# Second attention in a pipeline of four steps instead of three, and the work at its borders placed anew

## What is computed

```python
x = x + tanh(g_xattn[0]) * L0_xattn(layernorm(x), ctx)             # one head, softmax(q k^T / sqrt(128)) v
x = x + tanh(g_ffn[0])   * L0_ffn(layernorm(x), ...)               # 8 experts 128->256->128, relu, top 2 by softmax
x = x + tanh(g_xattn[1]) * L1_xattn(layernorm(x), ctx, ctx, mask)  # 16 heads of 8, biases, output projection
x = x + tanh(g_ffn[1])   * L1_ffn(layernorm(x), ...)               # 8 experts of 96 and a shared one, silu, top 2 by sigmoid
```

## Time and profile before

| | us |
|---|---|
| median of 3 runs | 766.39 (763.78, 766.39, 766.4) |
| the profiled execution | 767.7 |
| its span, first to last instruction | 765.9 |
| stage a | 0 to 136 |
| stage b | 136 to 376 |
| stage c | 376 to 616 |
| stage d | 616 to 765.9 |

### The profile page before, as it was taken

How to read it: one execution, slowest core, us unless ns; L and a number is a source line. 1 busy time by engine, 2 the same in 40 slices (tenths; PEclk the granted TensorE clock), 3 DMA queues, 4 the chain that set the end, 5 groups by cost and what they waited for, 6 DMA issues and landing times.

```text
span 765.9 us, 12807 instructions
## 1 busy us (share of the span) xinstructions
PE 649.0 (85%) x4078; PEld 503.5 (66%) x4078; DVE 560.2 (73%) x1281; ACT 426.0 (56%) x665; POOL 104.2 (14%) x133
## 2 busy tenths in 40 slices
PE   5865654979999999979599988988988489999996
PEld 3644443657787787757377666766756267888884
DVE  3567565687898898868478668668676669888885
ACT  3333321467777777756277666656766145555553
POOL 3444230020000000000401022022022100000000
PEclk8677665889999999999799999999999679999998
DMA  5312000000000000010244124224210000000000
GB/s 159 101 63 98 29 8 0 1 0 1 1 0 0 0 0 0 0 43 28 50 121 121 54 67 119 69 49 119 69 42 2 0 1 0 15 14 14 27 14 28
DMA packets 23698, 29.24 MB, mean 38 GB/s; under 512 B 3313, under 2 KB 17522, under 8 KB 23666
## 3 DMA queue, kind: packets, MB, share of 16 engines
q1 hardware_dynamic: 23666, 28.84, 13.1%
HBM read 19.99 MB, written 8.85 MB: 38 GB/s over the span
## 4 chain that ended last, share of the span: by engine, by line
PE 63%; DVE 18%; issue 6%; POOL 5%; ACT 5%; DMA 1%; DVEq 1%; SPq 0%; POOLq 0%; ACTq 0%
PE psum L371 12%; PE psum L373 11%; PE psum L372 11%; PE psum L1187 6%; PE psum L1202 3%; PE psum L1177 2%; DVE stats L281 2%; POOL rstd L293 2%; PE psum L360 2%; PE psum L1178 2%; DVE b_hl L811 2%; DVE xn L300 2%; DVE c_mx L1356 2%; PE psum L1503 2%; PE psum L319 1%
## 5 line engine op out<-in xcount | busy, mean ns | idle before, releaser
L371 PE MATMUL psum<-xh,w_hi 128*128 (+1 forms) x248 | 104.1, 420 | 5.2 <-DVE w_lo L1346 3.0
L1297 ACT ACTIVATE c_pt<-psum 77x512 f32<-77x512 f32 x128 | 74.5, 585 | 49.9 <-PE psum L1187 49.8
L372 PE MATMUL psum<-xl,w_hi 128*128 (+1 forms) x248 | 100.3, 404 | 0.0
L373 PE MATMUL psum<-xh,w_lo 128*128 (+1 forms) x248 | 100.1, 404 | 0.0
L930 ACT ACTIVATE b_hr<-psum,b1s 128x512 f32<-128x512 f32 x128 | 80.8, 686 | 24.0 <-PE psum L373 23.9
L978 DVE TENSOR_TENSOR b_hs<-b_hr,psum 128x1024 f32<-128x1024 f32 x64 | 77.9, 1217 | 21.7 <-ACT b_hr L930 20.4
L811 DVE TENSOR_TENSOR b_hl<-b_hs,b_hh 128x1024 fp32r<-128x1024 f32 x64 | 78.3, 1223 | 16.9 <-ACT b_hh L805 16.9
L805 ACT ACTIVATE b_hh<-b_hs 128x1024 fp32r<-128x1024 f32 x64 | 67.9, 1061 | 34.1 <-PE psum L373 32.2
L1187 PE MATMUL psum<-ident,c_pf 128*77 128x128 f32 x512 | 75.9, 286 | 0.0
L1187 PEld LDWEIGHTS psum<-ident,c_pf 128*77 128x77 f32 x512 | 59.4, 152 | 14.9 <-issue 10.4
L1302 ACT ACTIVATE c_pf<-c_sm,zero_col,exp_scale 128x616 f32<-128x616 f32 x64 | 57.3, 895 | 17.8 <-DVE c_sm L1362 17.8
(11 more groups left out here) (207 smaller groups left out, 1299.6 us busy)
## 6 DMA issues: line engine op xcount, KB each, us to landing
w_hi<-c_q_spread SPq DMA_DIRECT2D x24, 256.0 KB
stage<-in_weights SPq DMA_DIRECT2D x8, 576.0 KB, 4.2
c_q_spread<-w_hi SPq DMA_DIRECT2D x7, 512.0 KB, 3.4
ctxg<-in_ctxT SPq DMA_DIRECT2D x16, 156.0 KB, 4.1
c_k_spread<-w_lo SPq DMA_DIRECT2D x8, 312.0 KB, 2.2
x_all<-in_x SPq DMA_DIRECT2D x8, 256.0 KB, 2.7
out_dram<-x_all SPq DMA_DIRECT2D x8, 256.0 KB, 2.3
c_kb<-c_k_spread SPq DMA_DIRECT2D x48, 39.0 KB
```

Source lines behind the costliest of these rows:

```text
L371: pe.matmul(o, wh, h, start=start, stop=False)
L372: pe.matmul(o, wh, l, start=False, stop=False)
L373: return pe.matmul(o, wl, h, start=False, stop=stop)
L1297: a_.activation(pt[:, q % NC4, :], bank[2 + q % 2][0:S2, :], ACT.Copy).then_inc(pt_done, 1)
```

## The change

In stage c a fourth step is added: `step(a, m, t, u)`, u being the group before t. Turning the norm, high and low part, logits, their copy, turning and copy move from parts 13 to 15 of t to parts 1 to 6 of u. `project` goes ahead of the scores of part 9, `residual` to part 9, the statistics are divided over parts 11 (`dve_spread`) and 12 (`dve_moments`). `turn_out` waits in addition for the logits copy of the group before, since both use M1. In the last step but one `act_sigmoid` moves to part 6, `route.first` to part 7 and `route.second` to part 12; `route.weights` goes to part 2 of the last step. `pipeline4` writes out four steps ahead and three behind a loop of two turns; SP's and POOL's steps only take the fourth argument. In stage a, last step: the low part before `route.second`, and the late setup (with bank 5) on all three engines. In stage b, first step: the tail's routing in eight portions (two operations for `pick_part` 0 and 1, one for 2), the ratio at expert 6. In the last full step of stage b: the early preparation at experts 0 and 2 (PE) and 1 and 3 (ACT, DVE), y turned back and residual at 5, norm at 6; at the stage's end ACT copies the norm's high part before the values. No arithmetic is added or left out.

```diff
@@ -95,6 +95,19 @@
     step(None, None, Group(None, NG - 1))
+def pipeline4(eng, step):
+
+    def groups(i, c):
+        return [Group(i, c - k) if c - k >= 0 and (i is not None or c - k < NG) else None for k in range(4)]
+    for c in range(4):
+        step(*groups(None, c))
+    with eng.Fori(0, (NG - 4) // 2) as i:
+        step(*groups(i, 4))
+        step(*groups(i, 5))
+    for c in range(NG, NG + 3):
+        step(*groups(None, c))
+
+
 class Link:
@@ -284,6 +297,19 @@
                     ins = v.bn_aggr(m[:, p, t, :], st[:, p, t, :])
                 ins.then_inc(self.stats_ready, 1)
+            def dve_spread(self, v, g):
+                st, p = self.bufs[0], g.parity
+                for t in range(TG):
+                    ins = v.bn_stats(st[:, p, t, :], x_all[:, g.tile(t), :])
+                ins.then_inc(self.chain, 1)
+
+            def dve_moments(self, v, g):
+                st, m, p = self.bufs[0], self.bufs[1], g.parity
+                wait_apart(v, self.chain, g.at(1, 1))
+                for t in range(TG):
+                    ins = v.bn_aggr(m[:, p, t, :], st[:, p, t, :])
+                ins.then_inc(self.stats_ready, 1)
+
             def pool_rstd(self, q, g):
                 _, m, ve, rs, _ = self.bufs
                 p = g.parity
@@ -429,12 +455,12 @@
         def act_setup_late(a):
             a.wait_ge(s_m0, 2)
-            a.activation(bo_all[:], bank[7][:, 0:P], ACT.Copy, scale=tg[:, 1:2]).then_inc(s_m0e, 1)
+            a.activation(bo_all[:], bank[5][:, 0:P], ACT.Copy, scale=tg[:, 1:2]).then_inc(s_m0e, 1)
         def pe_setup_late(pe):
             pe.wait_ge(s_dve_setup, 1)
-            pe.matmul(bank[7][:, 0:P], bv1[:].broadcast_to([P, P]), wo1[:], start=True, stop=False)
-            pe.matmul(bank[7][:, 0:P], ones_row[:], bo1[:], start=False, stop=True).then_inc(s_m0, 1)
+            pe.matmul(bank[5][:, 0:P], bv1[:].broadcast_to([P, P]), wo1[:], start=True, stop=False)
+            pe.matmul(bank[5][:, 0:P], ones_row[:], bo1[:], start=False, stop=True).then_inc(s_m0, 1)
         def act_split(a_, a):
@@ -550,6 +576,8 @@
                     if t.i is None and t.c == 0:
                         pe.wait_ge(s_split, 1)
                     lg0.pe_product(pe, t)
+                    if not m:
+                        pe_setup_late(pe)
                     lg0.pe_transpose(pe, t)
             pipeline(pe, step)
         pe_parts.append(pe_a)
@@ -578,6 +606,7 @@
                 if t:
                     lg0.act_copy(a_, t)
                     if not m:
+                        act_setup_late(a_)
                         Route(0, HEAD, rt_tail).act_ratio(a_)
             pipeline(a_, step)
         act_parts.append(act_a)
@@ -614,7 +643,6 @@
                         v.wait_ge(s_small, 16 * len(small))
                         v.wait_ge(lg0.lg_copied, NG - 1)
                         route.first(v)
-                        route.second(v)
                 if a:
                     if not (a.i is None and a.c < 2):
                         v.wait_ge(ln0.t_ready, a.at(1, -1))
@@ -632,6 +660,8 @@
                 if t:
                     ln1.dve_low(v, t)
                     if not m:
+                        route.second(v)
+                        dve_setup_late(v)
                         route.weights(v)
                     lg0.dve_copy(v, t)
             pipeline(v, step)
@@ -664,15 +694,23 @@
...
+            def pick_part(self, v, k, values, best, onehot):
+                if k == 0:
+                    link(v, v.tensor_reduce(best, values, AX.X, ALU.max))
+                    link(v, v.tensor_tensor(rt["pick"][:], values, self.bc(best), ALU.is_ge))
+                if k == 1:
+                    link(v, v.tensor_tensor(rt["tmp"][:], rt["pick"][:], rankb, ALU.mult))
+                    link(v, v.tensor_reduce(r1["c"], rt["tmp"][:], AX.X, ALU.max))
+                if k == 2:
+                    link(v, v.tensor_tensor(onehot, rt["tmp"][:], self.bc(r1["c"]), ALU.is_equal))
+
+            def pick(self, v, values, best, onehot):
+
+                for k in range(3):
+                    self.pick_part(v, k, values, best, onehot)
...
@@ -890,18 +943,15 @@
                 for e in range(E if m else LAG):
                     if m:
                         up(m, e)
-                    if m and e == 4 and t:
+                    if m and e == (4 if a else 5) and t:
                         y_back(a, m, t)
                     g, k = xb.prev(m, t, e, LAG)
                     if g:
                         down(g, k)
-                    if m and not a and e < 2:
-                        c_prepare["pe"](pe, e)
+                    if m and not a and e in (0, 2):
+                        c_prepare["pe"](pe, e // 2)
                     if m and e == 2 and a:
                         place(a)
-                    if m and e == 5 and xb.first(m):
-                        pe.wait_ge(xb.st_done, 2)
-                        pe_setup_late(pe)
                     if m and e == 7 and t:
                         ln2.pe_transpose(pe, t)
                 if not m:
@@ -939,12 +989,10 @@
                         g, k = xb.prev(m, t, e)
                         if g:
                             xb.act_high(a_, g, k)
-                        if xb.first(m) and e == 3:
+                        if xb.first(m) and e == 6:
                             tail.act_ratio(a_)
-                        if xb.first(m) and e == 6:
-                            act_setup_late(a_)
-                        if not a and e in (1, 2):
-                            c_prepare["act"](a_, e - 1)
+                        if not a and e in (1, 3):
+                            c_prepare["act"](a_, e // 2)
                         if e == 3 and a:
                             xb.act_place(a_, a, MISC)
                         if e == 7 and t:
@@ -955,8 +1003,8 @@
                     if t:
                         xb.act_high(a_, t, E - 1)
                         xb.act_y(a_, t, Y)
+                        ln2.act_high(a_, t)
                         c_prepare["act"](a_, 2)
-                        ln2.act_high(a_, t)
             pipeline(a_, step)
         act_parts.append(act_b)
@@ -964,9 +1012,23 @@
             tail = Route(0, TAIL, rt_tail)
             def route_last(e):
-                if e == 1:
+                if e == 0:
                     v.wait_ge(lg0.lg_copied, NG)
-                (tail.first, tail.second, tail.weights)[e // 2](v)
+                    tail.values = logits[:, TAIL, :]
+                first = tail.values, tail.r1["m"], rt_tail["first"][:]
+                second = rt_tail["wt"][:], tail.r1["m2"], rt_tail["second"][:]
+                if e < 3:
+                    tail.pick_part(v, e, *first)
+                if e == 2:
+                    tail.mask_first(v)
+                if 3 <= e < 6:
+                    tail.pick_part(v, e - 3, *second)
+                if e == 5:
+                    tail.difference(v)
+                if e == 6:
+                    tail.shares(v)
+                if e == 7:
+                    tail.split(v)
             v.wait_ge(s_pool, 2)
@@ -991,16 +1053,14 @@
                             low(g, k)
                         if e == 0 and a:
                             xb.dve_place(v, a)
-                        if xb.first(m) and e in (1, 3, 5):
+                        if xb.first(m):
                             route_last(e)
-                        if xb.first(m) and e == 4:
-                            dve_setup_late(v)
-                        if not a and e in (1, 2):
-                            c_prepare["dve"](v, e - 1)
-                        if e == 4 and t:
+                        if not a and e in (1, 3):
+                            c_prepare["dve"](v, e // 2)
+                        if e == (4 if a else 5) and t:
                             xb.dve_residual(v, t, MISC)
                             ln2.dve_stats(v, t)
-                        if e == 5 and t:
+                        if e == (5 if a else 6) and t:
                             ln2.dve_norm(v, t)
                         if e == 7 and t:
                             ln2.dve_low(v, t)
@@ -1214,6 +1274,8 @@
             def turn_out(t):
                 pe.wait_ge(o_done, t.at(TG, TG))
+                if not (t.i is None and t.c == 0):
+                    pe.wait_ge(lg1.lg_copied, t.at(1, 0))
                 for b in range(TG):
...
@@ -1254,6 +1316,8 @@
                     g, q = lagged(m, t, i - 3)
                     if g:
                         transpose(g, q)
+                    if t and i == 9:
+                        project(t)
                     if m and i % 2 == 1 and i < NQ - 1:
                         scores(m, (i + 1) // 2)
                     if a and i == NQ - 1:
@@ -1262,16 +1326,14 @@
                         prepare(a, i // 3)
                     if a and m and i == 6:
                         prepare_values(a)
```

(57 more changed lines are left out.)

46 lines of the change are left out of this document (26 added, 20 removed).

## The result

The changed kernel takes 745.65 us (median of 6 runs, 743.24 to 748.15), the kernel before, run beside it, 765.21 (6 runs, 763.5 to 767.48). The ratio is 0.974 with a 95% interval of 0.971 to 0.977. The profiled execution of the changed kernel took 744.32 us with a span of 742.5, that of before 767.7 with 765.9.

The account below looks back on a forecast made before the run. TensorE (PE), busy 85% of the span, bounds the kernel through its pauses and lower clock. Gains 0 + 7.7 + 5.0 + 1.1 + 10.2 = 24.0 us gave 743.7, 742.4 against the median, 743.5 with one clock fall; range 736 to 753.

Parts of the forecast that it names:

- The likeliest case: Whole kernel: the main forecast of 743.5 us, given a chance of 0.62.
- End of stage a: Last step of the first attention: low part sooner, but PE waits for the moved setup; cost 0.2 us, taken as 0.
- an earlier rise of the clock: End of the first attention: PE busy without a pause from 134.0 may bring the clock up earlier, giving 0.6 us back.
- First expert step: Stage b's first step: without setup and bunched routing PE reaches the next group's first product at 160.8; gain 7.7 us.
- Rival (B): First expert step: DVE becomes the bound, half of the 7.7 us is lost, 747.4 us; chance 0.07.
- Last expert step and the border: End of stage b: PE's 2.99 us wait goes, gain 5.0; ACT's high part ahead of the values, gain 1.1 us.
- the new wait at the norm's turning: Last expert step: norm at expert 6 makes PE wait 1.6 us more at the turning of expert 7.
- Second attention: Stage c: full steps of 26.4 us, five taking 132.0 instead of 139.8; gain of the whole part 10.2 us.
- Rival (A): Second attention: full steps gain nothing, new stalls replace those removed; 752.5 us, chance 0.20 shared with Rival (C).
- Rival (C): Second attention: the clock falls in every step, six more falls of 1.4 us; 752 us, chance 0.20 shared with Rival (A).
- The 1.0 us that I added for one fall: Second attention: allowance of 1.0 to 1.4 us for one fall of the clock, raising the forecast to 743.5 us.

Follow-up runs that it names:

- e3: Changed kernel with the late setup put back into the first expert step, routing still in eight portions and the ratio at expert 6: 747.31 us, ratio 0.975.
- e4: Changed kernel with the tail's routing in three bunches again and ACT's ratio at expert 3, late setup kept at the end of stage a: 752.23 us, ratio 0.982.
- e9: Changed kernel with ACT copying the values ahead of the norm's high part again at the end of stage b: 748.57 us, ratio 0.977.
- e1: Changed kernel with the three-step stage c of the kernel before put back, border work in stages a and b kept: 758.62 us, ratio 0.990.
- e5: Changed kernel, still four steps, with residual and all statistics together at part 10 and the projection behind the scores of part 9: 746.07 us, ratio 0.975.
- e6: e1 with the split statistics, residual at 9 and projection ahead of part 9's scores, norm turning still in the same step: 783.49 us, ratio 1.023.
- e7: Changed kernel with stage c's low part, router product, logits copies, logits turning and sigmoid at later parts: 736.60 us, ratio 0.963.

## Why the prediction was right

The forecast was 743.5 us (736 to 753), measured were 745.65. The likeliest case came. In the profile, sections 2 to 6 give 23.2 us where the sum had 24.0; section 1, which the change does not touch, adds 0.7 by chance, and section 8 takes 0.5.

**End of stage a.** Right in the net: 0.55 us lost where I took 0, within the 0.9 us by which section 2 moves in equal kernels. The 0.6 us from an earlier rise of the clock did not come: the hidden products still ran at the lower clock up to 140.25. e3 shows that the net is made of two larger terms, about 2.5 gained and 3.1 lost.

**First expert step.** 7.64 us against 7.7. The product was walked to 160.8 and came at 160.74; the shares stood 0.5 us under the memset. Rival (B) was not so: DVE at 2.7 us an expert stayed under PE. What the walk did not tell is that either half left as it was keeps most of the cost: 6.14 us in e3, 4.95 + 2.42 in e4.

**Last expert step and the border.** 5.48 us against 6.1. e9 puts 1.15 on ACT's order, where 1.1 was predicted. The rest is 4.3 to 4.4 against 5.0: the new wait at the norm's turning was predicted at 1.6 and is 1.67, but two waits for low parts, 0.21 and 0.66 us, stand behind it, where I had let DVE follow at 1.13 us per operation without an effect on PE.

**Second attention.** 10.64 us against 10.2. From scores 1 of a full step the predicted starts were 2.9, 7.0, 11.8, 15.3, 18.06, 21.16, 23.7 and 26.4; the step of the rows above has 2.82, 7.08, 11.73, 15.29, 18.26, 21.21, 23.85 and 26.54. The stalls were predicted at 0.44, 0.89, 0.38 and 0.93 and are 0.44, 0.73, 0.42 and 0.62. The five full steps took 131.9 us against 132.0, the step of the first finished group 23.38 against 23.4. `turn_out` has no wait for the logits copy, and no scores wait for a DMA. Rival (A) was not so.

**The clock.** Rival (C) gave six falls. There was none: in the ten profiles of kernels with four steps all 50 full steps of stage c are free of it. (For one kind of step, the durations agree within 0.1 us from profile to profile.) With three steps, a fall followed 1.08 and 0.87 us of pause close together in two steps of five before and in four in e1. The step of the earlier trace rows has the same two pauses and no fall, so their size alone does not decide it. The pauses in the full steps of the changed kernel, 0.42 to 0.73 us and apart, never brought the clock down; the prediction had left this open, at a chance of 0.20 for (A) and (C) together. The Trainium skill (TensorE: Matmul & The Clock Gate, Part 1) says that idleness withdraws the clock. The traces agree in the direction. The 1.0 us that I added for one fall was too much for the profile.

**The 4 us between spans and medians.** Against the profile the working was close: 767.7 less 24.0 is 743.7, and 744.32 was measured. But the medians differ by 19.6 us only, where 22.9 were forecast (743.5 against 766.39), as the profile of before lies 2.5 us over its median and that of the changed kernel 1.3 us under its own. That the forecast time still met the measured one within 2.2 us owes 1.2 us to the kernel before, whose median was 765.21 beside the changed kernel and 766.39 when I predicted. One reason can be seen: the section ahead of mark 1, which the change doesn't touch, took 126.3 to 129.3 us in the twelve profiles of the tables and 126.77 in that of the changed kernel, near the shortest. Another is likely: the steps in which the clock falls differ from one execution of the three-step kernels to the next (e1's runs spread from 754.5 to 765.3). What the other runs lost where no trace tells, so this stays open.

## What to carry to other kernels

When a group's tail chain crosses three or four engines, give it to the next step of the pipeline, where other work lies between its links: that alone was worth the whole gain of stage c (e5; without it the rest costs time, e6). Then look at the stalls that are left inside the step: placing the links one or two parts later gave another 9 us (e7). Work out a step in starts from a fixed mark, per engine; and charge a wait of PE with the clock that may fall behind it, which cost more than the wait (e3: 2.0 us of wait, 3.1 us of clock).
